# One elementwise product per scan group in place of two in a Mamba and expert kernel

## What is computed

```python
def step(h, inp):
    d_t, B_t, C_t, u_t = inp
    dA = jnp.exp(d_t[..., None] * A)
    h = h * dA + (d_t * u_t)[..., None] * B_t[:, None, :]
    y = jnp.einsum('bdn,bn->bd', h, C_t)
    return (h, y)
```

## Time and profile before

| | |
|---|---|
| median of three runs | 901.2 us |
| profiled execution, its own time | 899.89 us |
| span of that execution, first to last instruction | 898.0 us |
| mean granted PE clock | 0.903 |
| DVE busy | 877.3 us (98%) |
| POOL busy | 795.4 us (89%) |
| PE busy | 746.1 us (83%) |
| ACT busy | 699.7 us (78%) |

### The profile page before, as it was taken

The page is one execution under the profiler, slowest core; times in us unless marked ns, Lnnn a source line. Parts: engine busy times, 40 slices in busy tenths (PEclk is TensorE's granted clock), DMA queues, the critical chain, the costliest instruction groups (busy, mean ns, idle before and its releaser), DMA issues.

```text
span 898.0 us, 10752 instructions
## 1 busy us (share of the span) xinstructions
PE 746.1 (83%) x3067; PEld 333.8 (37%) x3067; DVE 877.3 (98%) x631; ACT 699.7 (78%) x1191; POOL 795.4 (89%) x446
## 2 busy tenths in 40 slices
PE   8889877978889888799888987889878879889476
PEld 5334322332235444354443543445333432324122
DVE  6999999999999999999999999999999999999987
ACT  5999956865679889988989889997979977576550
POOL 0788789999999989889899988999898999999995
PEclk9969878796999989999899998989999899979579
DMA  7895353245545545553546636455554434453400
GB/s 235 228 281 120 110 118 109 91 106 159 149 112 171 130 160 146 183 134 101 181 116 192 165 72 211 124 185 130 182 139 111 135 87 169 106 172 69 103 0 13
DMA packets 90989, 123.60 MB, mean 138 GB/s; under 512 B 7978, under 2 KB 63275, under 8 KB 86963
## 3 DMA queue, kind: packets, MB, share of 16 engines
q1 hardware_dynamic: 88882, 118.72, 46.7%
q0 software_dynamic: 2048, 4.20, 1.5%
HBM read 75.57 MB, written 14.29 MB: 100 GB/s over the span
## 4 chain that ended last, share of the span: by engine, by line
issue 21%; POOL 15%; PE 10%; ACT 5%; DVE 3%; POOLq 0%; DMA 0%; ACTq 0%
POOL hs L1544 10%; POOL gu_w L1516 2%; PE front L607 2%; DVE hs L1305 2%; ACT L1099 2%; PE in_b L670 1%; PE y L704 1%; ACT dA L1090 1%; DVE in_b L1286 1%; POOL yg L1526 1%; PE y L695 1%; PE moe L860 1%; PE moe L878 1%; PE front L784 1%; DVE hs L1303 1%
## 5 line engine op out<-in xcount | busy, mean ns | idle before, releaser
L1544 POOL TENSOR_TENSOR hs<-hs,C_rep 128x1024 f32<-128x1024 f32 x255 | 596.1, 2358 | 43.3 <-DVE hs L1305 27.4
L1090 ACT ACTIVATE dA<-delta_rep,A_sb 128x511 f32<-128x511 f32 x512 | 335.7, 718 | 8.5 <-DMA delta_rep<-tmpA 5.3
L1286 DVE TENSOR_TENSOR in_b<-in_b,B_rep 128x1024 f32<-128x1024 f32 x256 | 300.7, 1222 | 6.0 <-PE in_b L670 5.4
L1305 DVE TENSOR_TENSOR_SCAN hs<-dA,in_b 128x1024 f32<-128x1024 f32 x128 | 285.4, 2271 | 0.4 <-PE y L704 0.4
L1303 DVE TENSOR_TENSOR_SCAN hs<-dA,in_b 128x1024 f32<-128x1024 f32 x128 | 285.3, 2273 | 0.1
L670 PE MATMUL in_b<-du,cst 128*128 128x512 f32 x256 | 156.9, 698 | 59.8 <-DVE hs L1305 44.9
L704 PE MATMUL y<-hs,cst 128*32 128x512 f32 x1016 | 133.3, 642 | 12.6 <-POOL hs L1544 12.5
L607 PE MATMUL front<-xpad,w_in 128*128 128x512 f32 x248 | 118.8, 614 | 8.1 <-ACT xi L1015 6.2
L1099 ACT ACT_TABLE_LOAD x71 | 91.1, 1283 | 13.3 <-PE moe L860 7.3
L670 PEld LDWEIGHTS in_b<-du,cst 128*128 128x128 f32 x256 | 46.6, 214 | 134.5 <-issue 131.0
L607 PEld LDWEIGHTS front<-xpad,w_in 128*128 128x128 f32 x248 | 46.8, 197 | 64.9 <-issue 50.9
(11 more groups left out here) (171 smaller groups left out, 816.7 us busy)
## 6 DMA issues: line engine op xcount, KB each, us to landing
delta_rep<-tmpA SPq DMA_DIRECT2D x126, 256.0 KB, 3.8
C_rep<-dbc_scratch SPq DMA_DIRECT2D x16, 1024.0 KB, 7.5
B_rep<-dbc_scratch SPq DMA_DIRECT2D x15, 1024.0 KB, 5.2
gu_w<-in_gate_up SPq DMA_DIRECT2D x39, 384.0 KB, 3.6
dn_w<-in_down SPq DMA_DIRECT2D x39, 192.0 KB, 2.9
xs<-sorted_tokens SPq DMA_DIRECT2D x39, 64.0 KB, 3.8
sorted_ffn<-ys SPq DMA_DIRECT2D x39, 64.0 KB, 2.6
sorted_tokens<-up_f SPq DMA_DIRECT2D x9, 256.0 KB, 4.6
```

The costliest lines, as they stand in the source:

```text
L1090: i = e.activation(dA[:, m % NA, r * L + 1:(r + 1) * L], src, ACT.Exp, scale=A_sb[:, d, 2 * p + jj, RH * rh + r:RH * rh + r + 1])
L1286: e.tensor_tensor(to, in_b[:, 2 + 2 * odd, :].unsqueeze(1).broadcast_to([P, RH, L]), by, ALU.mult).then_inc(dve_mult, 1)
L1305: e.tensor_tensor_scan(to[:, ::-1], a[:, 1:n + 1][:, ::-1], b[:, ::-1], 0.0, ALU.mult, ALU.add).then_inc(dve_scan, 1)
L1544: e.tensor_tensor(hs[:, m % NH, :], hs[:, m % NH, :], C_rep[:, u % 2, RH * rh:RH * rh + RH, :].rearrange("p r t -> p (r t)"), ALU.mult).th ...
```

## The change

Each group, save the very first, gets one product of 2048 elements in place of two of 1024. For it, du of an even group is spread into bank 0 and the product fills banks 3, 2, 1, 0 in this order; du of an odd group is spread into bank 4 and the product fills 1, 2, 3, 4. The scans stay two of 1024, and read banks 0 and 1, then 2 and 3 (even), or 1 and 2, then 3 and 4 (odd). The product waits for all scans of the group before, and both scans wait for the whole product. It raises `dve_mult` by 2. Group 0 keeps two products of 1024, in the other order: the second half of B is loaded first, and its product runs first. The last gate and sums use bank 0 in place of bank 2.

```diff
--- before.py
+++ after.py
@@ -430,7 +430,7 @@
                     e.wait_ge(dve_mult, NSTEP * (v - 1))
                     wait_c(e, NSTEP * (v - 1) - 1)
                 if v == 0:
-                    for h in range(2):
+                    for h in (1, 0):
                         e.dma_start(B_rep[:, 0, RH * h:RH * h + RH, :].rearrange("p r t -> p (r t)"),
                                     dbc_d[0, DR:DR + DS, :].rearrange("(g r) t -> g (r t)", g=G)
                                     [:, h * RH * L:(h + 1) * RH * L].unsqueeze(0).broadcast_to([DD, G, RH * L])
@@ -667,7 +667,7 @@
                 wait_du(e, v, j // 4)
                 if J * v + j >= 2:
                     e.wait_ge(dve_scan, 2 * (J * v + j - 1))
-                e.matmul(in_b[:, 2 + 2 * (j % 2), :], spread(j), du[:, du_slot(v, j // 4), :],
+                e.matmul(in_b[:, 4 * (j % 2), :], spread(j), du[:, du_slot(v, j // 4), :],
                          start=True, stop=True).then_inc(pe_du, 1)
 
             def first_pair(j):
@@ -725,7 +725,7 @@
                     n = LAST - 2 + r // RH
                     if r % RH == 0:
                         wait_c(e, n)
-                    i = e.matmul(in_b[r * DD:(r + 1) * DD, 2, :], sel, hs[:, n % NH, r % RH * L:(r % RH + 1) * L],
+                    i = e.matmul(in_b[r * DD:(r + 1) * DD, 0, :], sel, hs[:, n % NH, r % RH * L:(r % RH + 1) * L],
                                  start=True, stop=True, skip_group_check=True)
                 i.then_inc(pe_last_y, 1)
 
@@ -1265,26 +1265,23 @@
                                                moments[:, 0:1, :, 0], ALU.mult, ALU.mult)
                 o.then_inc(dve_shift, 1)
 
-            def du_B(m):
-
+            def du_B(m, rows=slice(0, R)):
 
                 u, s = divmod(m, NSTEP)
                 odd = s // 2 % 2
                 e.wait_ge(pe_du, J * u + s // 2 + 1)
-                if m < 2:
-                    e.wait_ge(in_half[m], 16)
+                if m == 0:
+                    e.wait_ge(in_half[rows.start // RH], 16)
                 elif s == 0:
                     wait_bc(e, u)
                 if m >= 2:
-                    e.wait_ge(dve_scan, m - 1)
-                if s % 2 == 0:
-                    to, by = in_b[:, 0:RH, :], B_rep[:, u % 2, 0:RH, :]
-                elif odd:
-                    to, by = in_b[:, 3:5, :], B_rep[:, u % 2, RH:R, :]
-                else:
-                    to, by = in_b[:, 2:4, :][:, ::-1, :], B_rep[:, u % 2, RH:R, :][:, ::-1, :]
-                e.tensor_tensor(to, in_b[:, 2 + 2 * odd, :].unsqueeze(1).broadcast_to([P, RH, L]), by,
-                                ALU.mult).then_inc(dve_mult, 1)
+                    e.wait_ge(dve_scan, m)
+                n = rows.stop - rows.start
+                to, by = in_b[:, odd + rows.start:odd + rows.stop, :], B_rep[:, u % 2, rows, :]
+                if not odd:
+                    to, by = to[:, ::-1, :], by[:, ::-1, :]
+                e.tensor_tensor(to, in_b[:, 4 * odd, :].unsqueeze(1).broadcast_to([P, n, L]), by,
+                                ALU.mult).then_inc(dve_mult, n // RH)
 
             def scan(m):
                 u, s = divmod(m, NSTEP)
@@ -1294,8 +1291,8 @@
                 if m == 0:
                     e.wait_ge(dve_wout, 1)
                 e.wait_ge(act_decay, m + 1)
-                e.wait_ge(dve_mult, m + 1)
-                low = (2 + odd) * half
+                e.wait_ge(dve_mult, m // 2 * 2 + 2)
+                low = odd + RH * half
                 n = RH * L
                 b = in_b[:, low:low + RH, :].rearrange("p r t -> p (r t)")
                 a, to = dA[:, m % NA, :], hs[:, m % NH, :]
@@ -1335,7 +1332,7 @@
                 e.wait_ge(act_four, 2)
                 for k in range(2):
                     n = slice(k * L // 2, (k + 1) * L // 2)
-                    e.tensor_tensor(yg_four[:, n], in_b[:, 2, n], z_four[:, n], ALU.mult).then_inc(dve_last_gate, 1)
+                    e.tensor_tensor(yg_four[:, n], in_b[:, 0, n], z_four[:, n], ALU.mult).then_inc(dve_last_gate, 1)
 
             def route(part):
 
@@ -1457,9 +1454,11 @@
                 for i in range(2):
                     if m >= R0:
                         route(2 * (m - R0) + i)
-                    if m < LAST and m % 2 == 0:
-                        du_B(m + i)
-                    elif m < LAST:
+                    if m == 0:
+                        du_B(0, slice(RH * (1 - i), RH * (2 - i)))
+                    elif i == 0 and m < LAST and m % 2 == 0:
+                        du_B(m)
+                    elif m < LAST and m % 2:
                         scan(m - 1 + i)
                 for x in C_ON_DVE:
                     if m % 2 and x in (m - 1, m):
```

## The result

The changed kernel took 943.01 us (median of 4 runs, 941.88 to 944.04) against 899.94 of the kernel before in the same comparison: ratio **1.0481, interval 1.0452 to 1.0511**. It is slower, as forecast, but by 43 us and not by 22, and outside the range of 916 to 930.

What follows compares the result with a forecast made beforehand. DVE was taken to bound the kernel. The profiled 899.89 us plus 23.8 for neighbours' waits net of the fusion's gain, less 1.5 of PE's lateness, gave 922.2 us; range 916 to 930.

Steps and rivals of the forecast that it cites:

- the bound: Whole recurrence: DVE, busy 98% of the span, sets the time; a change of its cost per group counts 127 times.
- the sign and its mechanism: DVE's groups: slower, +23.8 us before PE's give-back, as new waits on neighbours outweigh the fusion's gain; slower had chance 0.93.
- Forecast gain: One product for two on DVE: the fusion by itself gains only 0.056 us per group, most fixed part being already hidden.
- forecast product: DVE's product of 2048 elements: 2.284 us, from the rows at 512 and 1024; not over 2.444.
- the wait on a neighbour costs nothing: Rival, DVE's product and scans: the next instruction starts before the end although it waits; 7.1 us gained, 892.8; chance 0.05.
- the rule cited from the Trainium skill: DVE instructions: the next starts only once the pipe is empty, a semaphore costs nothing extra; 20 us gained, 880; no separate chance.
- A wait on the instruction directly ahead thus costs about 0.04 + 0.09 = 0.13 us: DVE, product to scan and scan to product: gap plus lost overlap, at 118 and 122 places, +8.7 and +15.5 us.
- The gap of 0.04: Between a DVE instruction's end and the start of the next one waiting for it: 0.04 us, bounds 0.03 to 0.05.
- B at the start: Group 0's load of B, second half first: the same wait of 0.48 us at the same place, so no cost.
- PE's lateness: DVE's waits for PE's spread of du, 5.4 us in five places: 0 to 5.4 comes back, 1.5 taken.
- the rival of the dear product: DVE's product over four banks costs two whole records, 2.444 us, adding 20 us: 942; chance 0.06.

Runs made afterwards that it cites:

- two_tight: Kernel before, still two products of 1024 per group, but with the changed kernel's waits on both scans and both products, each written last: 949.03 us, ratio 1.0577.
- last_one: Changed kernel with its waits in their own order, but each product raises dve_mult by 1 in place of 2: 942.08 us, ratio 1.0479.
- first_both: Changed kernel with only the wait order turned: dve_scan first in the product, dve_mult first in the scan: 925.00 us, ratio 1.0300.
- first_both_one: Changed kernel with the product's dve_scan wait and the scan's dve_mult wait written first, and each product raising dve_mult by 1: 920.57 us, ratio 1.0241.
- after_again: The changed kernel itself with no edit, timed again on the same chip as other runs: 943.49 us, ratio 1.0497.

## Why the prediction was right or wrong

**Right: the bound.** DVE sets the time, and period times groups gives it: from 6.615 to 7.07 us of period the time of every kernel whose scans read PSUM followed.

**Right: the sign and its mechanism.** The fusion by itself gains little, because the fixed part of an instruction lies mostly under its neighbour; a wait on the neighbour takes the overlap away. Forecast gain 0.056 a group, measured 0.07 by the starts and 0.054 by the time; forecast product 2.284 us, measured 2.300. The rival "the wait on a neighbour costs nothing" fell: 52 us in two_tight, which adds waits alone. A wait on the neighbour costs 0.13 us where the instruction carries it itself, and 0.18 to 0.23 where it does not. With that falls, for these instructions, the rule cited from the Trainium skill, "VectorE: DVE Perf Modes", section "The DRAIN you can't avoid", that a semaphore costs nothing extra. The prediction left out that the same section of the Trainium skill lets a next instruction that is not held back start earlier. So the overlap of 0.09 us agrees with that section, and it is the price of the wait that does not.

**Wrong: "A wait on the instruction directly ahead thus costs about 0.04 + 0.09 = 0.13 us".** The gap of 0.04, and its bounds of 0.03 to 0.05, came from the pairs of the earlier trace rows. In all of them the pending wait was the only one or the first written, and rode on the instruction. In the change the pending wait is the last of two or three. The runs show the rule for the product and the scan: the first wait written rides on the instruction, the others stand in a semaphore instruction ahead of it; the product that raises its semaphore by 2 carries none. If the one that is still pending stands there, the gap in the change is 0.13 by the starts (0.03, 0.05 and 0.04 in the chain); it is 0.10 to 0.11 where the semaphore instruction holds that wait alone (last_one, two_tight), and 0.09 to 0.10 ahead of the product of first_both, where it holds two. So 240 gaps of 0.13 in place of 0.04: 240 x 0.09 = 22 us, the size of the error (943 - 922 = 21). The smaller misses cancel: the product 127 x 0.016 = +2.0, B at the start +1.0, PE's lateness -3.6. The kernel that has the gaps I priced, first_both_one, took 920.6 against the 922.2 of the forecast, with 6.83 us a group against 6.82; that the times lie so close is in part luck, as there too the product's +2.0 and PE's -2.6 cancel.

The trace of before could have told it. The waits' lines have rows of their own there; L1297 is the scan's wait for `dve_mult` (count, ns min/median/max):

```profile
L1297 DVEq EVENT_SEMAPHORE  x256: 21/50/1734, 26.0 to 885.8; - x128
```

So every scan had a semaphore instruction ahead of it. These cost next to nothing there: all scans together stood idle for 0.5 us, so no table of waits named them.

**Near by luck, and wrong: the rival of the dear product.** Its 942 is close to the measured 943, but the product was 2.300 and not 2.444, which gives 2 us, not 20.

**Right, mis-sized: PE's lateness.** 1.5 of 5.4 us forecast to come back; 5.1 came back in the change, 3.8 in after_again, 4.1 in first_both_one. The longest wait, 2.3 us, which the forecast left standing, is not in these three profiles, where none is over 1.1 us.

None of the variants beats the kernel before. What the fusion has to give is 0.05 to 0.07 us a group, 7 to 9 us; two waits on a neighbour cost at least 0.25 us a group. With five banks for two groups the product cannot be put anywhere but next to the scans that it waits for; this is read from the layout, and no run tries another.

## What to carry to other kernels

On a saturated engine count an instruction by the start of the next one, not by its record, and ask of every wait that an edit adds whether it is on the direct neighbour. If it is, write it as the first of its instruction's waits, and let that instruction raise its own semaphore by 1, so that it carries the wait itself; in this kernel the two together were worth 23 us, the order alone 18. When a gap's price is taken from other rows, take it from rows whose waits are built the same way, not only from rows with the same dependence.

## What the runs showed of the hardware that was not expected

- The order in which an instruction's waits are written: 943.49 against 920.57 us for the same work (ratios 1.0497 and 1.0241), with a rise of 1 in place of 2 as the only other edit. The order alone gave 943 to 925.00; the rise alone gave 1.4 us, within the noise, and behind the turned order 4.4 us, with the period going from 6.89 to 6.83.
- A scan on DVE with both inputs in SBUF beside POOL's products from SBUF: median 3345 ns in place of 2273, and POOL's 4249 in place of 2357. With one input in PSUM, in the kernel before, the scans of L1303 stayed between 2256 and 2312 ns and POOL's products between 2330 and 2401, though DVE was busy 98% and POOL 89% of the span. The Trainium skill, "SBUF — State Buffer", section "Who interferes with whom", says that a DVE instruction with two SBUF inputs contends with a GpSimd (POOL) instruction that reads SBUF, while one with at most one SBUF input, outside the 2-port performance modes, does not; the runs agree. Some scans from SBUF still took 2258 ns, so the place of the operand is not slow in itself; which instruction held up which was not followed. The PSUM banks of `in_b` are thus more than a place for the matmul's result: moving the scan's input out of them cost 47% in this kernel.
